# Layer 2 linear attention: the reciprocals are applied channel-major, and the logits turned instead

## The chip, the cores and the metric

The kernel runs on one core of one Trainium2 chip. The metric is the device time of one execution in microseconds. The core's engines work side by side, each through its own list of instructions in order, and wait for each other on semaphores: TensorE (PE) multiplies matrices and turns tiles, VectorE (DVE), ScalarE (ACT) and GpSimd (POOL) work element by element, SyncE (SP) issues DMAs. "Bank" means a bank of PSUM, into which TensorE writes; all other tiles lie in SBUF.

## The reference, cut to what matters

The kernel computes four layers, each an attention-like part and a feed-forward part. The change lies in the attention part of layer 2, a gated linear attention with 64 memory slots: 16 heads, 64 key channels, 128 value channels, batch 4, 512 tokens after the kernel's grouping (B, T = 4, 512).

```python
def _chunk_abc(q, k, v, s):
    scale = q.shape[-1] ** (-0.5)
    z = jax.lax.cumlogsumexp(s, axis=2)
    g = jnp.exp(jnp.concatenate([z[:, :, :1], z[:, :, :-1]], axis=2) - z)
    p = jnp.exp(s - z)
    ...
    def step_k(hk, x):
        q_t, k_t, p_t, g_t = x
        hk = hk * g_t[:, :, None, :] + k_t[..., None] * p_t[:, :, None, :]
        return (hk, jnp.einsum('bhk,bhkm->bhm', q_t, hk))
    _, okT = jax.lax.scan(step_k, hk0, (qT, kT, pT, gT))
    pvT = jax.nn.softmax(okT, axis=-1)
    def step_v(hv, x):
        pv_t, v_t, p_t, g_t = x
        hv = hv * g_t[..., None] + p_t[..., None] * v_t[:, :, None, :]
        return (hv, jnp.einsum('bhm,bhmv->bhv', pv_t, hv))
    _, ovT = jax.lax.scan(step_v, hv0, (pvT, vT, pT, gT))
```

With e = exp(s) and c its running sum over the tokens, p and the product of the g's are quotients of e and c. So the logits of a token are (the causal sum of q.k times e of the earlier token) divided by c of its own, for each slot; a softmax over the 64 slots follows; its result, divided by c once more, weighs e and v of the earlier tokens.

## The kernel before, in words

`layer2_abc` does 32 units, u = 0 to 31: eight pairs of heads times four batches. A unit has 512 tokens in four chunks of 128, and its two heads lie side by side: 2 x 64 slots or channels are 128 rows. "Channel-major" tiles have slots or channels in the partitions and tokens in the columns, "token-major" ones the reverse.

In unit u, TensorE's list (`unit` in the tensor block, L1289) mixes the attention of unit u with the projections of unit u+1, which are long and wait for little, and with the output of unit u-1:

- `scores`: q.k for each chunk and head, to `pab`, masked by VectorE to `sm`.
- `chunk_sums`: for three chunks the product of `k_tok` and `e_tok` (to `pc`, a whole 128x128 for both heads, of which only the two 64x64 blocks are used) and of `e_tok` and v (to a ring bank, by heads in 64-row halves). VectorE adds them up from chunk to chunk: `prefix_k` makes `hk` in six steps, `prefix_v` makes `hv`.
- projections s, k, q of u+1, then `ok`: the logits' sums, token-major, in `pc`: from `hk` the past chunks, from `sm` the own chunk.
- `turn_out` of u-1 (the gated output turned), projections v0 and v1, `emit` of u-1 (its product with Wo, which VectorE adds into x at L1479), projection g0.
- `turn_w`: the softmax's result `wt`, turned to channel-major in `pc`, projection g1, `weights` (L1257: `wT` times `eT` to `pab`, masked to `am`; L1264: `wT` times `hv`), then the transposes `kt`, `et`, `rt` of u+1, and `ov` (the own chunk's values).

The running sum of `eT` is taken by VectorE (`project_c`), then the reciprocal in two halves of 256 columns in place (`project_r`, L1423). TensorE turns the result (`rt`) and ScalarE copies it to `r_tok`. Reciprocals are used twice, both times token-major: VectorE multiplies the logits by them (L1499), and GpSimd multiplies the exponentials by them (L1102), beside VectorE's sum of the exponentials. ScalarE copies the turned weights from `pc` to `wT`.

VectorE's list in unit u is: masks of the scores, `prefix_v`, the clipping of s, `prefix_k`, the gating of u-1, the copy of kT, the running sum, the three steps of the logits, sum and reciprocal of the softmax, its multiply, a half of the reciprocals, the addition into x, the other half, two gate products, the masks of `am`, the sum of squares. Everything is in the order of this code; there is no scheduler. Three PSUM banks (`ring`) serve eleven fills per unit in turn, in `before` by the number of the fill modulo 3; `ring_free` waits for who took the fill three places ahead.

Of the kernel before, what the change touches and what calls it, by code (L numbers as in the profile page):

```python
# [21 lines left out]
ALU = mybir.AluOpType  # L22
# [964 lines left out]
def layer2_abc(nc, st, core, dram, a, w, aT, w2):  # L987
# [25 lines left out]
    rT = st.sb("rT", [P, T])  # L1013
    k_tok, e_tok, r_tok = (st.sb(n, [P, 2, NCH, P]) for n in ("k_tok", "e_tok", "r_tok"))
# [17 lines left out]
             "c_ready r_ready v_copied tanh_ready gate_ready k_turned e_turned r_turned k_tok_ready e_tok_ready "  # L1032
             "r_tok_ready scores_ready sm_ready hk_sums hk_step ok_ready hv_sums hv_step zeros logit_step ex_ready "
             "er_ready den_step wt_ready w_turned wT_ready am_sums am_ready ov_ready sq_ready ms_step rstd_ready "
# [9 lines left out]
    FILL = {n: k for k, n in enumerate("s q k v0 v1 g0 g1 kt et rt hv".split())}  # L1044
    taken_by = ("s_clipped", "q_copied", "k_copied", "v_copied", "v_copied", "gate_ready", "gate_ready",
                "k_tok_ready", "e_tok_ready", "r_tok_ready", "hv_step")
    per_unit = {"v_copied": 2, "gate_ready": 2, "hv_step": 3, "v_ready": 2, "g_ready": 2, "tanh_ready": 2, "r_ready": 2}

    def bank(name):
        return ring[FILL[name] % 3]  # L1050

# [21 lines left out]
    with nc.Block() as block:  # L1073
# [15 lines left out]
        def _(pool):  # L1089
# [35 lines left out]
        def _(pe):  # L1125
            pe.wait_ge(s["zeros"], 1)

            def ring_free(name, u):


                n = FILL[name]
                if n >= 3:
                    by = taken_by[n - 3]
                    per = per_unit.get(by, 1)

                    step = 1 if n - 3 in (FILL["v0"], FILL["g0"]) else per
                    pe.wait_ge(s[by], per * u + step)
                else:
                    if isinstance(u, int) and u == 0:
                        return  # L1140
                    by = {0: "r_tok_ready", 1: "hv_step", 2: "e_tok_ready"}[n]
                    per = per_unit.get(by, 1)

                    pe.wait_ge(s[by], per * u)

            def project_rows(name, u, k):
# [6 lines left out]
                for c in range(DC):  # L1153
                    ins = split_matmul(pe, bank(name)[:],
                                       w_in_parts.view(lambda t: w_qks(t, slot)[:, FILL[name], c, :]),
                                       a.view(lambda t: t[:, c, b * T:(b + 1) * T]),
                                       start=(c == 0), stop=(c == DC - 1))
# [36 lines left out]
            def chunk_sums(u, k):  # L1194
# [34 lines left out]
            def ok(u, k):  # L1229
                pe.wait_ge(s["sm_ready"], 2 * (u + 1))  # L1230
                pe.wait_ge(s["hk_step"], 6 * (u + 1))
                tok4 = chunks(pc[:])
                for c in range(NCH):
                    if c:
                        pe.matmul(tok4[:, c, :], qT[:, k % 2, c * P:(c + 1) * P], hk[:, c - 1, :], start=True,
                                  stop=False, skip_group_check=True)
                    for h in range(2):
                        m = slice(DK * h, DK * h + DK)
                        ins = pe.matmul(tok4[:, c, m], sm[:, h, c, :], e_tok[:, k % 2, c, m], start=(c == 0),
                                        stop=True, skip_group_check=True)  # L1240
                ins.then_inc(s["ok_ready"], 1)

# [33 lines left out]
            def part(steps, u, k):  # L1276
                for x in steps.split():
# [6 lines left out]
                    elif x == "et":  # L1284
                        turn("et", eT[:, k % 2], "e_ready", "e_turned", u)
                    else:
                        turn("rt", rT[:], "r_ready", "r_turned", u)

            def unit(u, k, first, last):  # L1289
# [12 lines left out]
                project("v0 v1")  # L1302
# [7 lines left out]
                project("kt et rt")  # L1310
                ov(u, k)

            part("s q k v0 v1 g0 g1 kt et rt", 0, 0)
            rounds(pe, unit)
            pe.wait_ge(s["r_tok_ready"], HP * B)
# [8 lines left out]
        def _(act):  # L1324
# [28 lines left out]
            def project_turned(u, k, names):  # L1353
                for x, dst, n in (("kt", k_tok, "k"), ("et", e_tok, "e"), ("rt", r_tok, "r")):
# [7 lines left out]
            def unit(u, k, first, last):  # L1362
# [8 lines left out]
                act.wait_ge(s["logit_step"], 3 * (u + 1))  # L1371
# [20 lines left out]
            project_turned(0, 0, ("kt", "et", "rt"))  # L1392
# [9 lines left out]
        def _(dve):  # L1402
# [12 lines left out]
            def project_c(u, k):  # L1415

                dve.wait_ge(s["e_ready"], u + 1)
                dve.tensor_tensor_scan(rT[:], ones, eT[:, k % 2], 0.0, ALU.mult, ALU.add).then_inc(s["c_ready"], 1)

            def project_r(u, half):  # L1420
                cols = slice(half * (T // 2), (half + 1) * (T // 2))
                dve.wait_ge(s["c_ready"], u + 1)
                dve.reciprocal(rT[:, cols], rT[:, cols]).then_inc(s["r_ready"], 1)  # L1423
# [57 lines left out]
            def unit(u, k, first, last):  # L1481
# [13 lines left out]

                dve.wait_ge(s["ok_ready"], u + 1)
# [12 lines left out]
                dve.wait_ge(s["er_ready"], u + 1)  # L1509
# [2088 lines left out]
```

## Time and profile before

| | us |
|---|---|
| median of 3 runs | 2202.99 (2197.28 to 2205.3) |
| span of the profiled execution | 2195.6 |
| the 32 units of the stage, first to last `weights` | 572.2 to 1351.2 |

The profile page gives the span of the profiled execution, from its first to its last instruction; a time of its own around the span is not shown for it. The median of the runs is 7.4 us above this span, their lowest 1.7.

How to read the rows: a row of the timeline has the start in us from the span's start, the duration in us, the engine, the line of the kernel, the operation, the tile written and those read, the shape, and the number of merged instructions. A full-precision (f32) matmul appears as two records, so x16 are eight matmuls. `[0.54 <-DVE ...]` is idle time of the engine just before, and who ended it. The ends of matmuls are modelled and reach beyond the start of the next; on TensorE the distance between starts is what counts.

### The profile page before, as it was taken

What the parts mean: (1) busy time and instruction counts of PE and PEld (TensorE: products, weight loads), DVE (VectorE), ACT (ScalarE), POOL (GpSimd) and SP (SyncE); (2) the same over time, 40 slices, a digit from 0 to 9 for tenths busy, and PEclk for the clock granted to TensorE, in tenths of its full rate; (3) what the DMA queues carried; (4) which work ended last, traced back from release to release, by engine and by line L of the source; (5) the groups of instructions that cost most, each with busy time, mean ns of one, the idle gap of its engine ahead of it and who ended that gap; (6) DMA issues with size and microseconds to landing.
All of it is one profiled execution on the core that took longest, in us unless ns stands there. A gap on an engine that the chain in (4) does not pass through costs nothing. (4 is left out here: it accounts for less than half of the span.)

```text
span 2195.6 us, 35301 instructions
## 1 busy us (share of the span) xinstructions
PE 1903.1 (87%) x13120; PEld 1485.3 (68%) x13120; DVE 1384.1 (63%) x3005; ACT 710.9 (32%) x1269; POOL 610.0 (28%) x584
## 2 busy tenths in 40 slices
PE   5943669962999999999999997989997987989995
PEld 2341457741899999999999996455566876756663
DVE  4476445538777777777777776476656777533334
ACT  2231424431333333333333332235534323222221
POOL 0234725540131221222121312532332103401111
PEclk9975589985999999999999998999998996999997
DMA  9329234435000000000000100000001006111114
GB/s 324 122 75 294 83 112 150 141 113 161 1 1 23 1 23 23 1 23 1 23 1 23 32 1 1 1 1 2 2 1 51 27 1 240 69 37 48 45 47 134
DMA packets 100639, 134.96 MB, mean 61 GB/s; under 512 B 11616, under 2 KB 73980, under 8 KB 99968
## 3 DMA queue, kind: packets, MB, share of 16 engines
q1 hardware_dynamic: 89344, 102.16, 14.7%
q0 software_dynamic: 11136, 30.62, 3.9%
q8 instruction: 107, 1.75, 0.3%
q14 instruction: 52, 0.43, 0.1%
HBM read 81.94 MB, written 50.81 MB: 60 GB/s over the span
## 5 line engine op out<-in xcount | busy, mean ns | idle before, releaser
L1112 POOL TENSOR_TENSOR a_rstd<-a_ms,consts 128x8 f32<-128x8 f32 x32 | 52.3, 1635 | 384.2 <-DVE a_ms L1468 384.2
L110 PE MATMUL a_ring<-a_w_hi,l_xnT_hi 128*128 128x256 f32 x512 | 155.3, 303 | 0.0
L110 PE MATMUL a_ring<-a_w_hi,l_xnT_lo 128*128 128x256 f32 x512 | 144.7, 283 | 0.0
L110 PE MATMUL a_ring<-a_w_lo,l_xnT_hi 128*128 128x256 f32 x512 | 144.5, 282 | 0.0
L2455 POOL DMA_INDIRECT l_slots_in<-xn,f_row_of x96 | 102.7, 1069 | 93.6 <-DVE f_row_of L2749 36.9
L2982 POOL DMA_INDIRECT l_pairs_out<-f_yb,f_to_row x96 | 94.6, 985 | 101.0 <-ACT f_yb L2957 63.0
L1226 PE MATMUL a_pab<-a_w_o,a_oT 128*128 128x256 f32 x512 | 119.7, 389 | 2.4 <-ACT a_oT L1360 2.4
L1423 DVE RECIPROCAL a_rT<-a_rT 128x256 f32<-128x256 f32 x64 | 111.4, 1743 | 0.0
L1226 PEld LDWEIGHTS a_pab<-a_w_o,a_oT 128*128 128x128 f32 x512 | 100.7, 202 | 13.0 <-ACT a_oT L1360 3.2
L1467 DVE TENSOR_REDUCE a_ms<-a_on 128x8 f32<-128x1024 f32 x32 | 39.0, 1220 | 109.6 <-ACT a_on L1381 109.6
L1102 POOL TENSOR_TENSOR a_wt<-a_ex,a_r_tok 128x512 f32<-128x512 f32 x32 | 40.7, 1272 | 242.4 <-ACT a_ex L1372 242.4
L1703 PE MATMUL b_ring<-b_keys,b_qm 32*128 32x128 f32 (+2 forms) x896 | 91.5, 340 | 14.8 <-DVE b_nm L1916 9.4
L1869 ACT ACTIVATE b_work<-b_ring 128x1024 f32<-128x1024 f32 (+1 forms) x96 | 81.0, 881 | 62.3 <-PE b_ring L1710 61.3
L2876 PE MATMUL f_pgu<-f_gate_up_w,f_xT 128*128 x384 | 94.6, 390 | 7.4 <-ACT f_xT L2937 6.6
L3088 POOL DMA_INDIRECT l_pairs_out<-f_yb,f_to_row x40 | 38.4, 959 | 216.0 <-ACT f_yb L3170 216.0
L110 PEld LDWEIGHTS a_ring<-a_w_lo,l_xnT_hi 128*128 128x128 f32 x512 | 97.7, 191 | 0.8
L110 PEld LDWEIGHTS a_ring<-a_w_hi,l_xnT_hi 128*128 128x128 f32 x512 | 97.6, 191 | 0.6
L110 PEld LDWEIGHTS a_ring<-a_w_hi,l_xnT_lo 128*128 128x128 f32 x512 | 97.4, 190 | 0.0
L1703 PEld LDWEIGHTS b_ring<-b_keys,b_qm 32*128 32x128 f32 x896 | 65.4, 194 | 45.0 <-issue 21.2
L319 PE MATMUL n_turned<-consts,xn 128*128 128x128 f32 x96 | 24.9, 396 | 79.6 <-DVE xn L288 79.6
L3007 DVE TENSOR_TENSOR f_gu<-f_pgu,f_bias 128x256 f32<-128x256 f32 x96 | 40.8, 425 | 78.1 <-issue 46.6
L1350 ACT ACTIVATE a_th<-a_ring 128x512 f32<-128x512 f32 x64 | 38.2, 597 | 155.1 <-PE a_ring L110 155.1
(497 smaller groups left out, 5302.8 us busy)
## 6 DMA issues: line engine op xcount, KB each, us to landing
l_slots_in<-l_zeros SPq DMA_DIRECT2D x4, 3120.0 KB, 22.8
f_xb<-l_slots_in SPq DMA_DIRECT2D x11, 1040.0 KB
f_gate_up_w<-l_pairs_out SPq DMA_DIRECT2D x16, 512.0 KB, 8.7
l_slots_in<-l_zeros SPq DMA_DIRECT2D x4, 1300.0 KB, 15.8
f_xb<-l_slots_in SPq DMA_DIRECT2D x40, 130.0 KB
f_down_w<-L_ffn_w_down_dram SPq DMA_DIRECT2D x1, 4096.0 KB
f_gate_w<-L_ffn_w_dram SPq DMA_DIRECT2D x2, 2048.0 KB
f_up_w<-L_ffn_w_dram SPq DMA_DIRECT2D x2, 2048.0 KB
```

The costliest lines, as they stand in the source:

```text
L110: ins = pe.matmul(out, a, b, start=start and k == 0, stop=stop and k == 2, **kw)
L1102: pool.tensor_tensor(wt[:], ex[:], r_tok[:, k % 2], ALU.mult).then_inc(s["er_ready"], 1)
L1112: pool.tensor_tensor(rstd[:], ms[:], core.consts[:, C_HALF:C_HALF + 8], ALU.pow).then_inc(s["rstd_ready"], 1)
L1226: ins = pe.matmul(pyy[:, t, :], cols, w_o[:, slot, h, :], start=(h == 0), stop=(h == 1))
L1423: dve.reciprocal(rT[:, cols], rT[:, cols]).then_inc(s["r_ready"], 1)
L1467: do(dve.reduce_sum(ms[:], sq[:].rearrange("t h c v -> t (h c) v"), AX.X))
L1703: return pe.matmul(ps[:, i, at:at + k1 - k0], qm[strip(j), p, c, b * T + q * P:b * T + (q + 1) * P], keys[strip(j), p, c, b * T + k0:b * T ...
L1869: act.activation(probs[:, g % 2, 2 * pair:2 * pair + 2, T_AT[k]:T_AT[k] + w], slot["t", g, pair, k][:, :, 0:w], ACT.Exp).then_inc(s["exp_r ...
L2455: pool.indirect_dma_start(self.xs[:, :], bass.IndirectOffsetOnAxis(ap=self.row_of[:, k, t:t + 1], axis=0), core.rows[:, t, :], None).then_ ...
L2876: ins = pe.matmul(pgu[:, i % 2, j * 2 * I:(j + 1) * 2 * I], xT[:, i % 2, (j * DC + c) * P:(j * DC + c + 1) * P], r.gate_up[:, bass.ds(e, 1 ...
L2982: pool.indirect_dma_start(r.ys[:, :], bass.IndirectOffsetOnAxis(ap=r.to_row[:, b:b + 1], axis=0), yb[:, i % YR, j, :], None).then_inc(stor ...
L3007: dve.tensor_tensor(gu[:, i % GR, j].rearrange("p k i -> p (k i)"), pgu[:, i % 2, j * 2 * I:(j + 1) * 2 * I], r.bias[:, bass.ds(e, 1), :, ...
```

## The change

The reciprocals stay channel-major (`rT`, now in two buffers) and are never turned: `rt`, its copy and `r_tok` go. The logits are formed channel-major, so the operands of each product in `ok` change places; three products with `hk` come first, then eight half-width ones. VectorE multiplies the result by `rT` in this form (`lgT`), TensorE turns it back into `pc` (`turn_logits`, between v0 and v1), and the maximum and the subtraction read `pc`. GpSimd's multiply goes; the softmax's result is multiplied by the reciprocals only after it has been turned, by VectorE, in the place of ScalarE's copy to `wT`. The chunk sums of k are done by heads, 64x64 each. The ring banks are assigned by name.

```diff
@@ the banks
-    FILL = {n: k for k, n in enumerate("s q k v0 v1 g0 g1 kt et rt hv".split())}
+    BANK = {"hv": 0, "s": 1, "k": 2, "q": 0, "v0": 1, "v1": 2, "g0": 0, "g1": 1, "kt": 2, "et": 0}
+    BEFORE = {"s": ("gate_ready", 2, 0, 0), "k": ("k_tok_ready", 1, 0, 0), "q": ("hv_step", 3, 0, 0),
+              "v0": ("s_clipped", 1, 1, 1), "v1": ("k_copied", 1, 1, 1), "g0": ("q_copied", 1, 1, 1),
+              "g1": ("v_copied", 2, 1, 1), "kt": ("v_copied", 2, 2, 1), "et": ("gate_ready", 2, 1, 1)}
...
@@ gpsimd
-                pool.wait_ge(s["ex_ready"], u + 1)
-                pool.wait_ge(s["r_tok_ready"], u + 1)
-                pool.tensor_tensor(wt[:], ex[:], r_tok[:, k % 2], ALU.mult).then_inc(s["er_ready"], 1)
@@ tensor, chunk_sums
                 for c in range(3):
-                    ins = pe.matmul(pc[:, c * P:(c + 1) * P], k_tok[:, k % 2, c, :], e_tok[:, k % 2, c, :],
-                                    start=True, stop=True)
+                    for h in range(2):
+                        m = slice(DK * h, DK * h + DK)
+                        ins = pe.matmul(pc[m, c * P + DK * h:c * P + DK * h + DK], k_tok[:, k % 2, c, m],
+                                        e_tok[:, k % 2, c, m], start=True, stop=True)
@@ tensor, ok
-                tok4 = chunks(pc[:])
+                for c in range(1, NCH):
+                    pe.matmul(pc[:, c * P:(c + 1) * P], hk[:, c - 1, :], qT[:, k % 2, c * P:(c + 1) * P],
+                              start=(c == 1), stop=False, skip_group_check=True)
                 for c in range(NCH):
-                    if c:
-                        pe.matmul(tok4[:, c, :], qT[:, k % 2, c * P:(c + 1) * P], hk[:, c - 1, :], start=True,
-                                  stop=False, skip_group_check=True)
                     for h in range(2):
                         m = slice(DK * h, DK * h + DK)
-                        ins = pe.matmul(tok4[:, c, m], sm[:, h, c, :], e_tok[:, k % 2, c, m], start=(c == 0),
-                                        stop=True, skip_group_check=True)
+                        ins = pe.matmul(pc[m, c * P:(c + 1) * P], e_tok[:, k % 2, c, m], sm[:, h, c, :], start=False,
+                                        stop=(c == NCH - 1), skip_group_check=True)
                 ins.then_inc(s["ok_ready"], 1)
+
+            def turn_logits(u):
+                pe.wait_ge(s["lgT_ready"], u + 1)
+                for t in range(NCH):
+                    ins = pe.transpose(pc[:, t * P:(t + 1) * P], lgT[:, t * P:(t + 1) * P], core.ident)
+                ins.then_inc(s["lg_turned"], 1)
@@ tensor, unit
-                project("v0 v1")
+                project("v0")
+                turn_logits(u)
+                project("v1")
...
-                project("kt et rt")
+                project("kt et")
@@ scalar, unit
-                copy("w_turned", u + 1, wT[:], pc[:], "wT_ready")
...
-                    project_turned(n, kn, ("kt", "et", "rt"))
+                    project_turned(n, kn, ("kt", "et"))
@@ vector, unit
-                dve.wait_ge(s["r_tok_ready"], u + 1)
-                do = Steps(dve, s["logit_step"], 3 * u, 3)
-                do(dve.tensor_tensor(lg[:], chunks(pc[:]), r_tok[:, k % 2], ALU.mult))
-                do(dve.tensor_reduce(mx[:], heads8(lg[:]), AX.X, ALU.max))
-                do(dve.tensor_tensor(heads8(lg[:]), heads8(lg[:]), mx[:].unsqueeze(2).to_broadcast([P, 8, DK]),
+                dve.tensor_tensor(lgT[:], pc[:], rT[:, k % 2], ALU.mult).then_inc(s["lgT_ready"], 1)
+                if not last:
+                    project_r(n, kn, 0)
+                dve.wait_ge(s["lg_turned"], u + 1)
+                do = Steps(dve, s["logit_step"], 2 * u, 2)
+                do(dve.tensor_reduce(mx[:], heads8(chunks(pc[:])), AX.X, ALU.max))
+                do(dve.tensor_tensor(heads8(lg[:]), heads8(chunks(pc[:])), mx[:].unsqueeze(2).to_broadcast([P, 8, DK]),
                                      ALU.subtract))
...
-                dve.wait_ge(s["er_ready"], u + 1)
-                dve.tensor_tensor(heads8(wt[:]), heads8(wt[:]), den[:].unsqueeze(2).to_broadcast([P, 8, DK]),
+                dve.tensor_tensor(heads8(wt[:]), heads8(ex[:]), den[:].unsqueeze(2).to_broadcast([P, 8, DK]),
                                   ALU.mult).then_inc(s["wt_ready"], 1)
-                if not last:
-                    project_r(n, 0)
                 if not first:
                     emit(u - 1, (k - 1) % PER)
                 if not last:
-                    project_r(n, 1)
+                    project_r(n, kn, 1)
+                dve.wait_ge(s["w_turned"], u + 1)
+                dve.tensor_tensor(wT[:], pc[:], rT[:, k % 2], ALU.mult).then_inc(s["wT_ready"], 1)
+                if not last:
                     project_g(n, kn, 0)
                     project_g(n, kn, 1)
```

Where the instructions stand. TensorE in the middle of the stage, from `turn_w` to `turn_out`, of before (the projections, all of line L110, are left out here but for their place in the words behind):

```order
L1246 MATMUL a_pc<-consts,a_wt 128x128 x4
...
L1178 MATMUL a_ring<-consts,a_kT 128x128 x4
L1178 MATMUL a_ring<-consts,a_eT 128x128 x4
L1178 MATMUL a_ring<-consts,a_rT 128x128 x4
L1272 MATMUL a_pde<-a_v,a_am 128x128 x8
L1190 MATMUL a_pab<-a_qT,a_kT 128x128 x8
L1201 MATMUL a_pc<-a_e_tok,a_k_tok 128x128 x3
L1208 MATMUL a_ring<-a_v,a_e_tok 64x128 x6
```

The same place of the changed kernel, and on through `ok`, `turn_out` and the new turn of the logits:

```order
L1169 MATMUL a_ring<-consts,a_kT 128x128 x4
L1169 MATMUL a_ring<-consts,a_eT 128x128 x4
L1270 MATMUL a_pde<-a_v,a_am 128x128 x8
L1181 MATMUL a_pab<-a_qT,a_kT 128x128 x8
L1194 MATMUL a_pc<-a_e_tok,a_k_tok 64x64 x6
L1201 MATMUL a_ring<-a_v,a_e_tok 64x128 x6
...
L1226 MATMUL a_pc<-a_qT,a_hk 128x128 x3
L1231 MATMUL a_pc<-a_sm,a_e_tok 64x128 x8
L1210 MATMUL a_pde<-consts,a_on 128x128 x8
...
L1238 MATMUL a_pc<-consts,a_lgT 128x128 x4
```

The third turn is gone from between `et` and `ov`; a turn of the same size stands after the twelve matmuls of v0. VectorE from the running sum to the gate products, of before:

```order
L1418 SCALAR_TENSOR_TENSOR a_rT<-consts,a_eT 128x512
L1499 TENSOR_TENSOR a_lg<-a_pc,a_r_tok 128x512
L1500 TENSOR_REDUCE a_mx<-a_lg 128x8
L1501 TENSOR_TENSOR a_lg<-a_lg,a_mx 128x512
L1506 TENSOR_REDUCE a_den<-a_ex 128x8
L1507 RECIPROCAL a_den<-a_den 128x8
L1510 TENSOR_TENSOR a_wt<-a_wt,a_den 128x512
L1423 RECIPROCAL a_rT<-a_rT 128x256
L1479 TENSOR_TENSOR x<-a_pab,x 128x1024
L1423 RECIPROCAL a_rT<-a_rT 128x256
L1428 SCALAR_TENSOR_TENSOR a_gate<-a_th,a_ring 128x512 x2
```

The same in the changed kernel:

```order
L1415 SCALAR_TENSOR_TENSOR a_rT<-consts,a_eT 128x512
L1496 TENSOR_TENSOR a_lgT<-a_pc,a_rT 128x512
L1421 RECIPROCAL a_rT<-a_rT 128x256
L1501 TENSOR_REDUCE a_mx<-a_pc 128x8
L1502 TENSOR_TENSOR a_lg<-a_pc,a_mx 128x512
L1507 TENSOR_REDUCE a_den<-a_ex 128x8
L1508 RECIPROCAL a_den<-a_den 128x8
L1510 TENSOR_TENSOR a_wt<-a_ex,a_den 128x512
L1477 TENSOR_TENSOR x<-a_pab,x 128x1024
L1421 RECIPROCAL a_rT<-a_rT 128x256
L1517 TENSOR_TENSOR a_wT<-a_pc,a_rT 128x512
L1426 SCALAR_TENSOR_TENSOR a_gate<-a_th,a_ring 128x512 x2
```

The first half of the reciprocals moved ahead of the maximum, and the multiply that fills `wT` stands behind the second half and ahead of the gate products.

## Rows read from the trace of the kernel before

**Rows 1.** Busy time by stretch: busy us (instructions) by engine, clock, DMA.

```profile
570.00:1350.00 780.00, 775.00 (x6336) 711.57 (x6336) 584.29 (x943) 266.89 (x406) 179.37 (x101) 0.99 0.04 12
1338.00:1347.00 9.00, 7.80 (x32) 6.95 (x32) 7.41 (x22) 1.63 (x2) 1.91 (x2) 0.50 0.00 0
1450.00:1600.00 150.00, 134.88 (x1784) 83.55 (x1788) 100.16 (x142) 79.61 (x99) 44.58 (x113) 0.99 0.01 2
```

**Rows 2.** Timeline of TensorE, first matmuls of `weights` in units 1 and 30.

```profile
597.31 1.16 PE L1257 MATMUL a_pab<-a_wT,a_eT 64*128 64x128 f32 x16
...
1325.56 1.16 PE L1257 MATMUL a_pab<-a_wT,a_eT 64*128 64x128 f32 x16
```

**Rows 3.** Timeline of TensorE, 940 to 966 us, a unit in the middle.

```profile
942.04 3.62 PE L1226 MATMUL a_pab<-a_w_o,a_oT 128*128 128x256 f32 x16
...
946.92 0.60 PE L1246 MATMUL a_pc<-consts,a_wt 128*128 128x128 f32 x4
...
948.87 1.16 PE L1257 MATMUL a_pab<-a_wT,a_eT 64*128 64x128 f32 x16
...
951.56 0.60 PE L1178 MATMUL a_ring<-consts,a_rT 128*128 128x128 f32 x4
952.00 1.95 PE L1272 MATMUL a_pde<-a_v,a_am 128*128 128x128 f32 x16
953.88 1.16 PE L1190 MATMUL a_pab<-a_qT,a_kT 64*128 64x128 f32 x16
954.97 0.94 PE L1201 MATMUL a_pc<-a_e_tok,a_k_tok 128*128 128x128 f32 x6
955.84 0.88 PE L1208 MATMUL a_ring<-a_v,a_e_tok 128*64 128x128 f32 x12
956.64 0.51 PE L110 MATMUL a_ring<-l_xnT_hi,a_w_hi 128*128 128x512 f32 x1
...
960.92 0.63 PE L1239 MATMUL a_pc<-a_e_tok,a_sm 128*128 128x64 f32 x4
961.39 0.44 PE L1235 MATMUL a_pc<-a_hk,a_qT 128*128 128x128 f32 x2
...
963.40 1.05 PE L1217 MATMUL a_pde<-consts,a_on 128*128 128x128 f32 x8
964.20 0.36 PE L110 MATMUL a_ring<-a_w_hi,l_xnT_hi 128*128 128x256 f32 x1
```

**Rows 4.** Timeline of VectorE, the same stretch.

```profile
939.99 0.69 DVE L1501 TENSOR_TENSOR a_lg<-a_lg,a_mx 128x512 f32<-128x512 f32 x1
...
943.36 0.69 DVE L1510 TENSOR_TENSOR a_wt<-a_wt,a_den 128x512 f32<-128x512 f32 x1 [0.42 <-POOL a_wt L1102]
...
945.70 1.22 DVE L1479 TENSOR_TENSOR x<-a_pab,x 128x1024 f32<-128x1024 f32 x1
946.84 1.74 DVE L1423 RECIPROCAL a_rT<-a_rT 128x256 f32<-128x256 f32 x1
948.50 0.63 DVE L1428 SCALAR_TENSOR_TENSOR a_gate<-a_th,a_ring 128x512 f32<-128x512 f32 x1
...
955.04 1.22 DVE L1467 TENSOR_REDUCE a_ms<-a_on 128x8 f32<-128x1024 f32 x1 [3.55 <-ACT a_on L1381]
...
959.78 0.99 DVE L1458 TENSOR_TENSOR a_hk<-a_pc,a_hk 64x64 f32<-64x64 f32 x4
...
963.68 0.67 DVE L1499 TENSOR_TENSOR a_lg<-a_pc,a_r_tok 128x512 f32<-128x512 f32 x1
```

**Rows 5.** Timeline of all engines: before unit 0, and in unit 31.

```profile
554.94 0.66 PE L1178 MATMUL a_ring<-consts,a_rT 128*128 128x128 f32 x4 [0.54 <-DVE a_gate L1428]
...
1335.88 0.99 DVE L1458 TENSOR_TENSOR a_hk<-a_pc,a_hk 64x64 f32<-64x64 f32 x4
...
1337.01 0.78 PE L1239 MATMUL a_pc<-a_e_tok,a_sm 128*128 128x64 f32 x4 [3.61 <-DVE a_hk L1458]
```

More of the change, by code:

```diff
@@ L1012, in layer2_abc @@
     qT, kT, eT = (st.sb(n, [P, 2, T]) for n in ("qT", "kT", "eT"))
-    rT = st.sb("rT", [P, T])
-    k_tok, e_tok, r_tok = (st.sb(n, [P, 2, NCH, P]) for n in ("k_tok", "e_tok", "r_tok"))
+    rT, lgT = st.sb("rT", [P, 2, T]), st.sb("lgT", [P, T])
+    k_tok, e_tok = (st.sb(n, [P, 2, NCH, P]) for n in ("k_tok", "e_tok"))
     v, gate = (st.sb(n, [P, 2, NCH, PV]) for n in ("v", "gate"))
@@ L1128, in ring_free @@
             def ring_free(name, u):
[L1131 to L1136, printed above, removed]
-                    pe.wait_ge(s[by], per * u + step)
[L1138 to L1144, printed above, removed]
+                by, per, step, own = BEFORE[name]
+                if own or u:
+                    pe.wait_ge(s[by], per * u + step)
             def project_rows(name, u, k):
@@ L1283, in part @@
                         turn("kt", kT[:, k % 2], "k_copied", "k_turned", u)
-                    elif x == "et":
+                    else:
                         turn("et", eT[:, k % 2], "e_ready", "e_turned", u)
-                    else:
-                        turn("rt", rT[:], "r_ready", "r_turned", u)
             def unit(u, k, first, last):
@@ L1309, in unit @@
                 weights(u, k)
-                project("kt et rt")
+                project("kt et")
                 ov(u, k)
-            part("s q k v0 v1 g0 g1 kt et rt", 0, 0)
+            part("s q k v0 v1 g0 g1 kt et", 0, 0)
             rounds(pe, unit)
-            pe.wait_ge(s["r_tok_ready"], HP * B)
+            pe.wait_ge(s["gate_ready"], 2 * HP * B)
             for t in rn.of(0):
@@ L1353, in project_turned @@
             def project_turned(u, k, names):
-                for x, dst, n in (("kt", k_tok, "k"), ("et", e_tok, "e"), ("rt", r_tok, "r")):
+                for x, dst, n in (("kt", k_tok, "k"), ("et", e_tok, "e")):
                     if x in names:
@@ L1370, in unit @@
                     project_v(n, kn, 0)
-                act.wait_ge(s["logit_step"], 3 * (u + 1))
+                act.wait_ge(s["logit_step"], 2 * (u + 1))
                 act.activation(ex[:], lg[:], ACT.Exp).then_inc(s["ex_ready"], 1)
@@ L1391, in _ @@
             project_g(0, 0, 1)
-            project_turned(0, 0, ("kt", "et", "rt"))
+            project_turned(0, 0, ("kt", "et"))
             rounds(act, unit)
@@ L1417, in project_c, with project_r @@
                 dve.wait_ge(s["e_ready"], u + 1)
-                dve.tensor_tensor_scan(rT[:], ones, eT[:, k % 2], 0.0, ALU.mult, ALU.add).then_inc(s["c_ready"], 1)
-            def project_r(u, half):
+                dve.tensor_tensor_scan(rT[:, k % 2], ones, eT[:, k % 2], 0.0, ALU.mult, ALU.add
+                                       ).then_inc(s["c_ready"], 1)
+            def project_r(u, k, half):
                 cols = slice(half * (T // 2), (half + 1) * (T // 2))
                 dve.wait_ge(s["c_ready"], u + 1)
-                dve.reciprocal(rT[:, cols], rT[:, cols]).then_inc(s["r_ready"], 1)
+                dve.reciprocal(rT[:, k % 2, cols], rT[:, k % 2, cols]).then_inc(s["r_ready"], 1)
             def project_g(u, k, half):
@@ L1527, in _ @@
             project_c(0, 0)
-            project_r(0, 0)
-            project_r(0, 1)
+            project_r(0, 0, 0)
+            project_r(0, 0, 1)
             project_g(0, 0, 0)
```

14 lines of the change are left out of this document (7 added, 7 removed).

## The prediction

> **What bounds the kernel now.** I read four views: the table of stretches for the whole layer 2 attention stage, one line's starts from unit to unit, then TensorE's rows and VectorE's rows of one unit in the middle. The stretches say what sets the pace [rows 1]: from 570 to 1350 us TensorE is busy 775.0 of 780.0 us at a granted clock of 0.99, that is the 2.4 GHz level, VectorE 584, ScalarE 267, GpSimd 179. The starts of the `weights` matmuls say how steady it is [rows 2]: 597.31 for unit 1, 1325.56 for unit 30, so 29 periods in 728.25 us, 25.11 us each. A unit's wait or saving therefore counts some 30 times (unit 0 to unit 30), and the ends by themselves.
>
> I write W for the start of `weights` in a unit (948.87) and give times as W plus something. TensorE's rows [rows 3] stand back to back: W+3.13 turn of `rT` ends (952.00), W+5.01 `ov` ends, W+12.05 `ok` starts, W+14.53 it ends, W+18.28 `emit` starts (942.04 plus a period), W+25.11 next W. VectorE [rows 4] runs without a gap from the sum of squares (955.04) to the logits, and has idle time elsewhere. Two places where it nearly holds TensorE: its last `hk` step ends at 960.77 and `ok` starts at 960.92. In the last unit, where TensorE really waits for that step, the start comes 0.14 us after it (1336.87 to 1337.01) [rows 5], so the 0.15 here is the same latency: `ok` starts when VectorE lets it, and TensorE arrives at the same moment. The other place is `emit`: its last matmul ends at 945.66, VectorE's addition into x starts at 945.70, 0.04 us later.
>
> **The change, part by part, per unit.**
>
> *Reciprocals not turned.* Four transposes go from TensorE: 951.56 to 952.00, 0.44 us, before `ov`, so all that follows moves up by 0.44, VectorE's chain too, since that starts from `ov`. The ScalarE copy of them goes too, on an engine with two thirds of its time free: nothing.
>
> *Chunk sums in 64-column tiles.* Three full matmuls took 0.87 us (954.97 to 955.84); six half ones take between half of the neighbouring `hv` sums' 0.80 us (six matmuls with 128 moving columns) and all of it, and one change of tile shape goes: 0.1 to 0.4 us less. It is worth nothing on the path: `ok` waits for the `hk` step, which is 0.14 us behind a VectorE chain that starts at ScalarE's squares and runs without a gap; TensorE only waits a little at `ok`. The bound on the other side: 0.1 us a unit if the 0.14 is not all latency.
>
> *Logits formed channel-major.* Before, 960.92 to 963.40, 2.48 us, with the weights of 64-column products loaded in full width and three switches to the `hk` products. Now three full products and eight that write half the output partitions. The full ones at the rate of `ov`, 1.88 us for eight (952.00 to 953.88), cost 0.70. The half ones have exactly the shape of the `hv` sums, 128*64 by 128x128, whose six take 0.80, change of shape behind them included; two more at the pace inside a run, 0.11 each, give 1.02, and the change ahead of them about 0.09. Sum 1.81, saving 0.67. Bounds: 1.6 if no change of shape costs, 2.6 if the halves do not overlap (8 x 0.235 + 0.70).
>
> *Logits turned back.* Four transposes, priced like those removed: 0.44, added between `v0` and `v1`. What they wait for: VectorE's multiply starts where the old one did, W+14.81, less 0.44, at W+14.37, since the scan ahead of it is the binding thing. It takes 0.67 from PSUM as the old one did, so the turn may start at W+15.1. TensorE gets there at 11.61+1.81+0.80 (`turn_out`)+1.48 (half of the 2.95 us of `v0 v1`) = W+15.70. No wait, with 0.6 us of cover.
>
> *The softmax chain.* Behind the multiply now stands half the reciprocals (1.74), then the maximum and the subtraction from PSUM, 0.69 us each as the present ones: subtraction done by 15.04+1.66+0.72+0.72, about W+18.1. The old distance from there to the weights' multiply was 2.68 us (940.68 to 943.36) and held GpSimd's product, for which VectorE waited 0.42 at the end; the product goes. Even at the old distance `wt` is done at W+21.5 (18.1+2.68+0.69), and `turn_w` stands at 23.17 (946.92 plus a period) less 0.67, W+22.5. One microsecond of cover. So the freed GpSimd work is worth nothing either.
>
> *The second multiply by the reciprocals, at `wT`.* This is where the saving is lost. The copy of the turned weights leaves ScalarE, where it ran beside VectorE's reciprocals, and becomes a VectorE multiply that stands behind the addition into x and the second half of the reciprocals. The addition can't start before `emit` is done. From the end of the last `emit` matmul: 0.04 to the addition, 1.14 to the reciprocals behind it (945.70 to 946.84), 1.66 to the next instruction (946.84 to 948.50), 0.67 for the multiply from PSUM, 0.14 to TensorE: 3.65 us. TensorE's own work from that point to `weights` is 948.87 less 945.66, 3.21 us. It waits 0.44 us in every unit. What is queued behind it on TensorE is all the next unit needs; behind the multiply on VectorE stand the two gate products and the masks of `am`. Two gates and one mask at 0.69 each, from the multiply's end at W'-0.14, give W'+1.9 for the first mask, `ov` asks for it at W'+2.69 (952.00 less 948.87 less the 0.44): covered.
>
> The Trainium skill, "VectorE: DVE Perf Modes", section on the TRN2 errata, gives VectorE 120 cycles of fixed cost from PSUM against 58 from SBUF, an argument against this move. The rows contradict it: 0.67 us from PSUM (963.68), 0.69 from SBUF alone (943.36), the same 512 elements. By the page's difference (62 cycles, an estimate of 0.06 us over the SBUF row) the wait would be about 0.53 and the time about 2198.
>
> **The sum.** TensorE's own work changes by -0.44 - 0.67 + 0.44 = -0.67 and it waits 0.44: -0.23 us a unit, over 30 periods -6.9. At the start the turn of `rT` waited for the gate, 0.54 idle and 0.66 of its own at 554.94 [rows 5], and goes: 1.2 us. Unit 0 begins those 1.2 and the 0.67 of `ok` earlier, but has no `emit` to hide VectorE's softmax chain, which has half the reciprocals more (1.66) and the wait for GpSimd less (0.42): -1.2 - 0.67 + 1.66 - 0.42 = -0.6. In the last unit VectorE sets most of the end as before; I give it -0.1. Together -7.6 us on the profiled execution's 2195.6 us span. The page shows no other time of that execution; the median of three runs is 7.4 us above its span, so I carry the difference over: 2203.0 - 7.6 = 2195.4.
>
> **Rivals.**
> *No wait at `wT`.* If the addition into x or the reciprocals start 0.44 us sooner than the rows let them, all of 0.67 stays: 30 x 0.67 + 0.7 = 21 us, 2182. For it: 0.44 us in a chain of five terms is not much, and the two latencies stand on one row each. Against: the three long terms are durations of this trace, in a row, on an in-order engine.
> *The half-width products don't overlap, slower than before.* In `ok` both halves accumulate onto a bank that the full-width `hk` products have begun. If such pairs run one behind the other, `ok` takes 2.6 to 2.7 us, 0.85 more than forecast, and the period is 25.11 - 0.23 + 0.85: 30 x 0.62 - 0.7 = +18, 2221. It becomes slower than before from an `ok` of about 2.05 us up. For it: the shape has not been seen with accumulation in this kernel. Against: the `hv` sums write one bank in halves, six in 0.80 us, while full products of the same size take 0.235 each.
> *The clock.* In the last unit the clock fell to 0.50 (the 1.2 GHz level) after 3.61 us without work [rows 1, 5]. If 0.44 us a unit did that, every unit would lose some 4 us. Against: from 1450 to 1600 us TensorE idles 15 of 150 us, at 0.99 [rows 1].
> *More waits on VectorE.* If the multiply of the logits came 0.6 us later than computed, the turn would wait too; each 0.1 beyond costs 3 us.
>
> **How the numbers follow.** Forecast 0.64, its own range 2190 to 2199. No wait 0.16. Pairs in series 0.10. Clock or a further wait 0.10, of which half stays within the next bound. Three runs of a kernel here span 8 us, so about 0.5%, 11 us, is what can be told from no change. Faster by more than that: the no-wait case and a fifth of all for a forecast whose wait is half as long, 0.36. Slower: pairs in series and most of the last case, 0.17. Within: 0.47. The range leaves out a tenth on either side: 2181 to 2208.
>
> **What would show it.** The period of the `weights` line: 24.88 us. TensorE idle before `weights`, ended by VectorE's `wT` multiply, 0.4 us in each unit; no such idle at the turn of the logits. `ok` from its first `hk` product to `turn_out` 1.8 us. A small wait at `ok` on `hk`, as long as the chunk sums got shorter. The multiply at `wT` 0.67 us, starting as the second half of the reciprocals ends. Clock 0.99 throughout. Wrong if `ok` lasts over 2 us, if `wT` does not come last before `weights`, or if the wait stands at `turn_logits`.

## The result, and the profile after

| | before | after |
|---|---|---|
| median of 4 runs, us | 2203.99 (2197.28 to 2205.3) | 2192.93 (2190.69 to 2193.66) |
| span of the profiled execution, us | 2195.6 | 2192.1 |
| period of a unit, us | 25.11 | 24.84 |

The ratio of the times is 0.9949, 95% interval 0.9936 to 0.9962: 11 us faster, about 8 to 14. Forecast was 2195.4, within 2181 to 2208.

The two spans differ by 3.5 us only, and that needs a word first. The time of an execution of either kernel lies 1.5 to 1.7 us above its own span (the profiled one of after: 2193.66 against 2192.1). So the profiled execution of the kernel before, with its span of 2195.6, fits its fastest time, 2197.28, and most of the 7.4 us between that span and the median is scatter between executions. The stage with the change (from the load of the norm's weights to the first instruction of the next stage) took 836.5 us before and 825.6 after, 10.9 less. But the stage began at 541.2 us in the trace of before and at 549.2 in that of after, behind layers that the change doesn't touch. Over all ten kernels profiled for this case the start lies between 541 and 556 us whatever the edit (table below). So a comparison of two traces goes by the stage, never by the span. The same scatter widens the intervals of the first four experiments: of 27 executions of the kernel before that ran beside them, eight took 2195.7 to 2199.9 us and nineteen 2204.5 to 2214.3.

The table of stretches of the kernel after, whole stage and last unit (columns as in rows 1):

```profile
577.00:1345.00 768.00, 744.43 (x6509) 669.33 (x6508) 595.96 (x970) 236.81 (x343) 140.22 (x70) 0.99 0.04 13
1335.00:1344.00 9.00, 8.54 (x40) 7.08 (x41) 6.93 (x19) 1.67 (x2) 1.64 (x1) 0.50 0.00 0
```

TensorE is no longer busy all the time: 23.6 us of 768 are idle, where it was 5.0 of 780 [rows 1]. The clock is the same, 0.99, the 2.4 GHz level. The first `weights` matmuls of units 1 and 30:

```profile
603.59 1.16 PE L1255 MATMUL a_pab<-a_wT,a_eT 64*128 64x128 f32 x16 [0.24 <-DVE a_wT L1517]
...
1323.94 1.16 PE L1255 MATMUL a_pab<-a_wT,a_eT 64*128 64x128 f32 x16 [0.23 <-DVE a_wT L1517]
```

29 periods in 720.35 us, 24.84 each, against 25.11 [rows 2], and each of the two rows has the idle time that the prediction asked for, ended by VectorE's `wT` multiply, though it is 0.24 us and not 0.4. TensorE in a unit in the middle:

```profile
951.35 1.16 PE L1255 MATMUL a_pab<-a_wT,a_eT 64*128 64x128 f32 x16 [0.24 <-DVE a_wT L1517]
...
954.04 1.95 PE L1270 MATMUL a_pde<-a_v,a_am 128*128 128x128 f32 x16
955.92 1.16 PE L1181 MATMUL a_pab<-a_qT,a_kT 64*128 64x128 f32 x16
957.01 0.57 PE L1194 MATMUL a_pc<-a_e_tok,a_k_tok 128*64 128x64 f32 x12
957.41 0.83 PE L1201 MATMUL a_ring<-a_v,a_e_tok 128*64 128x128 f32 x12
958.17 0.50 PE L110 MATMUL a_ring<-l_xnT_hi,a_w_hi 128*128 128x512 f32 x1
...
962.96 0.91 PE L1226 MATMUL a_pc<-a_qT,a_hk 128*128 128x128 f32 x6 [0.38 <-DVE a_hk L1456]
963.79 1.09 PE L1231 MATMUL a_pc<-a_sm,a_e_tok 128*64 128x128 f32 x16
964.82 1.09 PE L1210 MATMUL a_pde<-consts,a_on 128*128 128x128 f32 x8
965.67 0.36 PE L110 MATMUL a_ring<-a_w_hi,l_xnT_hi 128*128 128x256 f32 x1
...
967.18 0.60 PE L1238 MATMUL a_pc<-consts,a_lgT 128*128 128x128 f32 x4
...
969.04 3.62 PE L1219 MATMUL a_pab<-a_w_o,a_oT 128*128 128x256 f32 x16
...
973.92 0.60 PE L1244 MATMUL a_pc<-consts,a_wt 128*128 128x128 f32 x4
...
976.18 1.05 PE L1255 MATMUL a_pab<-a_wT,a_eT 64*128 64x128 f32 x14 [0.24 <-DVE a_wT L1517]
```

Times from W = 951.35, beside those of [rows 3]: `ov` ends at 4.57 (5.01), `ok` starts at 11.61 (12.05), ends at 13.47 (14.53), `emit` starts at 17.69 (18.28), next W at 24.83 (25.11). The chunk sums take 0.40 us (957.01 to 957.41) where they took 0.87, and `ok` starts exactly as far from `ov` as it did, 7.04 us: the time saved there has become a wait of about half a microsecond, of which the row shows 0.38 as idle. There is none at the turn of the logits (967.18). VectorE in the same unit:

```profile
961.82 0.99 DVE L1456 TENSOR_TENSOR a_hk<-a_pc,a_hk 64x64 f32<-64x64 f32 x4
...
965.72 0.66 DVE L1496 TENSOR_TENSOR a_lgT<-a_pc,a_rT 128x512 f32<-128x512 f32 x1
966.30 1.74 DVE L1421 RECIPROCAL a_rT<-a_rT 128x256 f32<-128x256 f32 x1
967.96 0.63 DVE L1501 TENSOR_REDUCE a_mx<-a_pc 128x8 f32<-128x512 f32 x1
968.62 0.69 DVE L1502 TENSOR_TENSOR a_lg<-a_pc,a_mx 128x512 f32<-128x512 f32 x1
...
971.03 0.69 DVE L1510 TENSOR_TENSOR a_wt<-a_ex,a_den 128x512 f32<-128x512 f32 x1
972.70 1.23 DVE L1477 TENSOR_TENSOR x<-a_pab,x 128x1024 f32<-128x1024 f32 x1 [0.97 <-PE a_pab L1219]
973.84 1.74 DVE L1421 RECIPROCAL a_rT<-a_rT 128x256 f32<-128x256 f32 x1
975.50 0.63 DVE L1517 TENSOR_TENSOR a_wT<-a_pc,a_rT 128x512 f32<-128x512 f32 x1
```

The three VectorE instructions behind `emit` read as the prediction wrote them [rows 4 for before]: the addition at 972.70 after 0.97 idle, reciprocals at 973.84 (1.14 later), the multiply at 975.50 (1.66 later), 0.63 long, and TensorE starts at 976.18. The multiply of the logits starts at W+14.37, as forecast.

### The profile page after: what moved, and what is told of

Same layout as the page of the kernel before. It is cut to its first block and busy times, and to the rows that moved or that the text cites. A ratio compares the mean times of both kernels' runs of the same rounds, so it can differ in the third digit from the quotient of the medians.

```text
span 2192.1 us, 35525 instructions
## 1 busy us (share of the span) xinstructions
PE 1875.1 (86%) x13312; PEld 1444.0 (66%) x13312; DVE 1399.3 (64%) x3037; ACT 680.2 (31%) x1205; POOL 565.3 (26%) x552
## 5 line engine op out<-in xcount | busy, mean ns | idle before, releaser
L110 PE MATMUL a_ring<-a_w_hi,l_xnT_hi 128*128 128x256 f32 x512 | 157.3, 307 | 0.0
L110 PE MATMUL a_ring<-a_w_hi,l_xnT_lo 128*128 128x256 f32 x512 | 144.2, 282 | 0.0
L110 PE MATMUL a_ring<-a_w_lo,l_xnT_hi 128*128 128x256 f32 x512 | 144.0, 281 | 0.0
L110 PEld LDWEIGHTS a_ring<-a_w_lo,l_xnT_hi 128*128 128x128 f32 x512 | 97.2, 190 | 0.8
L110 PEld LDWEIGHTS a_ring<-a_w_hi,l_xnT_hi 128*128 128x128 f32 x512 | 97.0, 189 | 0.8 <-issue 0.2
L110 PEld LDWEIGHTS a_ring<-a_w_hi,l_xnT_lo 128*128 128x128 f32 x512 | 96.8, 189 | 0.0
L1711 PE MATMUL b_ring<-b_qm,b_keys 32*128 32x384 f32 (+3 forms) x512 | 86.9, 461 | 0.0
## 6 DMA issues: line engine op xcount, KB each, us to landing
f_gate_w<-L_ffn_w_dram SPq DMA_DIRECT2D x2, 2048.0 KB, 11.1
```

Of the source, the lines that this page charges most:

```text
L110: ins = pe.matmul(out, a, b, start=start and k == 0, stop=stop and k == 2, **kw)
L1711: return pe.matmul(ps[:, i, at:at + T - kb * P], keys[strip(j), p, c, b * T + kb * P:b * T + (kb + 1) * P], qm[strip(j), p, c, b * T + kb ...
```

## The experiments

All kernels are compared with the kernel before. after_again, e1, e4 and e2 ran together on one chip, e5, e3, e6 and e7 together on another. The start and length of the stage and the period (the distance between two `weights`, mean of 29) are read from each kernel's trace, in us. But for e5's, the intervals of the ratios overlap, so the conclusions rest on period and stage.

| kernel | stage starts | period | stage | time, us | ratio to before |
|---|---|---|---|---|---|
| before | 541.2 | 25.11 | 836.5 | | |
| after | 549.2 | 24.84 | 825.6 | 2192.9 | 0.9949 (0.9936 to 0.9962) |
| after_again | 555.2 | 24.84 | 825.3 | 2196.9 | 0.9954 (0.9924 to 0.9984) |
| e1_r_ahead | 541.9 | 24.53 | 815.9 | 2188.9 | 0.9925 (0.9896 to 0.9954) |
| e4_clip_behind | 555.5 | 24.29 | 808.4 | 2182.8 | 0.9901 (0.9865 to 0.9938) |
| e2_full_sums | 549.3 | 24.84 | 826.6 | 2198.4 | 0.9962 (0.9933 to 0.9991) |
| e5_both | 548.6 | 23.99 | 799.1 | 2167.9 | 0.9835 (0.9822 to 0.9849) |
| e3_before_half_sums | 548.5 | 25.13 | 837.4 | 2205.3, one run | |
| e6_wT_first | 549.3 | 24.77 | 823.4 | 2192.6, one run | |
| e7_pool | 549.3 | 24.85 | 825.7 | 2193.9, one run | |

**The changed kernel again** (after_again), no edit.

> The changed kernel once more, as the measure for the others of this chip. Period of the weights line 24.84 us as before in its trace, the stage from its first DMA to the next stage's first instruction 825.7 us. Open: its total against the kernel before. The stage alone is 10.9 us shorter in the two traces, while the spans differ by 3.5 us only, because the changed kernel's stage began 8.1 us later. If the late start was chance, the ratio comes out near 0.995 again; if the change causes it (another place of code or tiles), the stage starts late again, near 549 us, in this trace and the ratio stays near 0.998 to 0.995.

Period 24.84, stage 825.3, ratio 0.9954. The late start doesn't come from the change: e3, the kernel before with one edit, starts at 548.5, and e1, with the change, at 541.9. What lies behind the stage is 817 to 818 us in nine of the ten traces (815 in e2), so in the traces it is the part ahead of the stage that varies. TensorE spent 207 us of that part at the lower level of its clock (0.50) in the two traces that start the stage earliest, 214 to 227 in the six that start it near 549, and 225 and 240 in the two near 555. The two go together, though not in strict order; which is the cause isn't shown. The waits of TensorE in this kernel, over 22 units (who waited, for whom, us in total, times, longest):

```profile
PEld a_pab L1255 <- DVE a_wT L1517: 9.6, 22, 0.4
PE a_pc L1226 <- DVE a_hk L1456: 8.4, 22, 0.4
...
PE a_pab L1255 <- DVE a_wT L1517: 5.2, 22, 0.2
```

**The second half of the reciprocals ahead of the addition** (e1_r_ahead).

```diff
-                if not first:
-                    emit(u - 1, (k - 1) % PER)
                 if not last:
                     project_r(n, kn, 1)
+                if not first:
+                    emit(u - 1, (k - 1) % PER)
                 dve.wait_ge(s["w_turned"], u + 1)
```

> The changed kernel with the second half of the reciprocals ahead of the addition into x on VectorE, nothing else. Theory (TensorE waits 0.30 us a unit at weights because addition, reciprocals and the multiply stand in a row on VectorE behind emit): the reciprocals fill the 0.97 us in which VectorE idles before the addition, the multiply ends about 0.9 us earlier, the wait at weights goes, period 24.53 to 24.56, about 9 us less than the changed kernel. Rival (the gap at weights is a fixed cost, a change of tile shape or semaphore latency behind g1): period stays 24.84, time the same. Second rival (the addition, 0.7 us later, now holds weights, which waits for it too): period 24.9 or more.

Period 24.53, the theory's number; the stage 9.3 to 9.7 us shorter than in the two traces of the changed kernel, the median 8 us lower. Two successive `weights` rows, no idle time ahead of either:

```profile
939.84 1.16 PE L1255 MATMUL a_pab<-a_wT,a_eT 64*128 64x128 f32 x16
...
964.37 1.16 PE L1255 MATMUL a_pab<-a_wT,a_eT 64*128 64x128 f32 x16
```

And of the two waits only the one for `hk` is left in the list of waits:

```profile
PE a_pc L1226 <- DVE a_hk L1456: 9.5, 23, 0.4
```

So the gap at `weights` was the row of work on VectorE, 0.31 us of it in each unit, neither a fixed cost of TensorE nor the addition alone. The multiply itself got no faster; it stands behind the addition now and takes 0.69 us where it took 0.63:

```profile
963.06 0.69 DVE L1517 TENSOR_TENSOR a_wT<-a_pc,a_rT 128x512 f32<-128x512 f32 x1
```

**Clipping behind the hk steps** (e4_clip_behind).

```diff
+                prefix_k(u)
                 if not last:
                     project_s(n, kn)
-                prefix_k(u)
```

> The changed kernel with the clipping of s behind the six hk steps on VectorE instead of ahead of them. Theory (the shorter chunk sums are lost at ok, where TensorE waits 0.5 us for hk): the hk steps end 0.61 us earlier, ok starts 0.45 to 0.5 us earlier, period 24.34 to 24.40, about 14 us less than the changed kernel. The wait at weights stays at 0.30, since emit moves with it. Rival (ok waits for something else, the masks or the projections): period 24.84. Rival that gives a part back: the exponential and the running sum come later, the multiply of the logits too, and TensorE waits at the turn of the logits: period 24.5 to 24.8.

Period 24.29, 0.55 less, a little more than expected; stage 17 us shorter, the median 14. The start of `ok` moves from W+11.61 to W+11.08. The wait at `ok` is gone from the list, the one at `weights` stays:

```profile
PE a_pab L1255 <- DVE a_wT L1517: 5.4, 23, 0.2
```

The queue ahead of `hk` on VectorE was what `ok` waited for. The same queue stood there in the kernel before; it cost nothing visible, because TensorE arrived at the same moment.

**Full chunk sums** (e2_full_sums), the change without one of its parts.

```diff
                 for c in range(3):
-                    for h in range(2):
-                        m = slice(DK * h, DK * h + DK)
-                        ins = pe.matmul(pc[m, c * P + DK * h:c * P + DK * h + DK], k_tok[:, k % 2, c, m],
-                                        e_tok[:, k % 2, c, m], start=True, stop=True)
+                    ins = pe.matmul(pc[:, c * P:(c + 1) * P], k_tok[:, k % 2, c, :], e_tok[:, k % 2, c, :],
+                                    start=True, stop=True)
```

> The changed kernel with the chunk sums of k as before, three full 128x128 products. Theory (halving them is hidden by the hk steps): TensorE's chunk sums take 0.87 us instead of 0.40, the start of ok moves by 0.05 at most, period 24.84 to 24.90, time the same within 2 us. Rival (the halved sums made the gain): period 25.3, 14 us slower than the changed kernel and about the time of the kernel before.

Period 24.84, unchanged, and the median within the 2 us (2198.4 against 2196.9). The rows of one unit (start at W = 952.86): the sums take 0.87 again, and `ok` starts at W+11.61 as with the halved ones, without idle time ahead of it.

```profile
952.86 1.16 PE L1253 MATMUL a_pab<-a_wT,a_eT 64*128 64x128 f32 x16 [0.23 <-DVE a_wT L1515]
...
958.52 0.94 PE L1192 MATMUL a_pc<-a_e_tok,a_k_tok 128*128 128x128 f32 x6
959.39 0.88 PE L1199 MATMUL a_ring<-a_v,a_e_tok 128*64 128x128 f32 x12
...
964.47 0.91 PE L1224 MATMUL a_pc<-a_qT,a_hk 128*128 128x128 f32 x6
```

**Halved chunk sums alone in the kernel before** (e3_before_half_sums), the same edit the other way round, by itself.

> The kernel before with one part of the change alone, the chunk sums of k by heads as 64x64 products. Theory (ok of the kernel before starts 0.14 us after the last hk step, which is this wait's latency, so it is VectorE that sets it): TensorE's chunk sums take 0.40 us instead of 0.87, it waits the difference at ok, period 25.05 to 25.12. Rival (TensorE was the bound there, the two coincided by chance and the latency is shorter, 0.05 us): up to 0.1 us less, 25.01. Rival (halving is a gain by itself): 24.65.

Period 25.13, 0.02 more than before and 0.01 above the theory's range. The sums are 0.5 us shorter and `ok` waits for VectorE, W+12.06 (W+12.05 before):

```profile
956.51 1.16 PE L1259 MATMUL a_pab<-a_wT,a_eT 64*128 64x128 f32 x16
...
962.61 0.57 PE L1203 MATMUL a_pc<-a_e_tok,a_k_tok 128*64 128x64 f32 x12
...
968.57 0.63 PE L1241 MATMUL a_pc<-a_e_tok,a_sm 128*128 128x64 f32 x4 [0.41 <-DVE a_hk L1460]
```

Together with e2 this settles that part of the change: it is worth nothing in either kernel. The kernel before was held by VectorE at this point, by a hair.

**Both moves** (e5_both): the edits of e1 and e4 together in the changed kernel.

> The changed kernel with both moves: the clipping of s behind the hk steps, and the second half of the reciprocals ahead of the addition into x. Theory (two separate waits, 0.3 us at weights and 0.5 us at ok, one VectorE queue behind each): the gains add, period 24.84 - 0.31 - 0.55 = 23.98, up to 24.1, stage 25 us shorter than the changed kernel's 825.5, some 800, and about 37 us less than the kernel before. Rival (the waits are one, moved about: TensorE then waits for VectorE at a third place, the turn of the logits or the turn of the softmax's weights): period 24.2 to 24.3, no better than the better one of the two alone.

Period 23.99, stage 799.1; ratio 0.9835 to the kernel before, 37 us faster. The savings add up (24.84 - 0.31 - 0.55 = 23.98), so the two waits were separate. TensorE's rows of one unit, two `weights` and what is between them at the places of the former waits, without idle time:

```profile
938.45 1.16 PE L1255 MATMUL a_pab<-a_wT,a_eT 64*128 64x128 f32 x16
...
944.51 0.83 PE L1201 MATMUL a_ring<-a_v,a_e_tok 128*64 128x128 f32 x12
...
949.49 0.89 PE L1226 MATMUL a_pc<-a_qT,a_hk 128*128 128x128 f32 x6
...
962.44 0.83 PE L1255 MATMUL a_pab<-a_wT,a_eT 64*128 64x128 f32 x10
```

Here the halved chunk sums should count, though no run has them full in this kernel: the 4.98 us from the `hv` sums to `ok` (944.51 to 949.49) are their own 0.76 and the 4.22 of the projections. TensorE sets the pace again, but barely: `ok` starts 0.17 us after the last `hk` step ends (948.33 + 0.99 = 949.32), where 0.15 was the distance when it had to wait.

**The multiply at wT ahead of the second half** (e6_wT_first).

```diff
-                if not last:
-                    project_r(n, kn, 1)
                 dve.wait_ge(s["w_turned"], u + 1)
                 dve.tensor_tensor(wT[:], pc[:], rT[:, k % 2], ALU.mult).then_inc(s["wT_ready"], 1)
                 if not last:
+                    project_r(n, kn, 1)
                     project_g(n, kn, 0)
```

> The changed kernel with the second half of the reciprocals behind the multiply that fills wT, instead of ahead of it. Theory (the wait at weights is the row addition, half reciprocals, multiply): the multiply is done before TensorE asks, the wait at weights goes, but the 1.66 us stand ahead of the gate products and the masks now, the first mask ends 2.9 us after weights begins or later, and ov, which asks for it at 2.69, waits 0.2 to 0.5 us. Period 24.7 to 25.0: the wait has moved. Rival (masks have cover enough): period 24.53, as with the reciprocals ahead of the addition.

Period 24.77, within the theory's range: `ov` starts at W+2.83 instead of 2.69, and lasts 0.10 longer for its second mask, 0.24 in all (24.53 + 0.24 = 24.77). The wait has moved, as the list shows; VectorE waits for the turned weights, and TensorE's weight loads for the mask:

```profile
DVE a_wT L1515 <- PE a_pc L1244: 14.7, 23, 0.6
...
PEld a_pde L1270 <- DVE a_am L1433: 4.6, 22, 0.2
```

**GpSimd's multiply back, without use** (e7_pool).

```diff
+                pool.wait_ge(s["ex_ready"], u + 1)
+                pool.wait_ge(s["e_tok_ready"], u + 1)
+                pool.tensor_tensor(lg[:], ex[:], e_tok[:, k % 2], ALU.mult).then_inc(s["idle_done"], 1)
...
                 dve.wait_ge(s["lg_turned"], u + 1)
+                if not first:
+                    dve.wait_ge(s["idle_done"], u)
```

> The changed kernel with GpSimd's multiply of 512 columns put back without use: it multiplies ex by e_tok and writes the result over lg, which nobody reads again. Theory (GpSimd's work was off the path and doesn't slow VectorE beside it): period 24.83 to 24.85, VectorE's sum of the exponentials beside it 0.69 us as now. Rival (part of the gain comes from a quieter GpSimd, through the memory they share): VectorE's instructions beside it longer by some per cent, and the period 24.9 or more.

Period 24.85, 0.01 more, as the theory said. But the other half of the theory, that GpSimd doesn't slow VectorE beside it, holds for one instruction and fails for the next:

```profile
971.82 1.27 POOL L1107 TENSOR_TENSOR a_lg<-a_ex,a_e_tok 128x512 f32<-128x512 f32 x1 [7.83 <-ACT a_ex L1373]
...
971.84 0.69 DVE L1512 TENSOR_REDUCE a_den<-a_ex 128x8 f32<-128x512 f32 x1 [0.76 <-ACT a_ex L1373]
...
972.80 0.84 DVE L1515 TENSOR_TENSOR a_wt<-a_ex,a_den 128x512 f32<-128x512 f32 x1
974.47 1.22 DVE L1480 TENSOR_TENSOR x<-a_pab,x 128x1024 f32<-128x1024 f32 x1 [0.83 <-PE a_pab L1222]
```

The sum, which lies wholly beside GpSimd's multiply, takes its usual 0.69 us. The multiply behind it, which overlaps GpSimd's by 0.3 us, takes 0.84 instead of 0.69 (0.836 to 0.847 in all 32 units). That costs no time here, because VectorE idles ahead of the addition: 0.83 us where it was 0.97. In the kernel before, this multiply waited for GpSimd's and could not overlap with it. So GpSimd's work was off the path in this change, but not without an effect on VectorE; in the order of e5, where VectorE doesn't idle there, it might count. That wasn't run.

## Why the prediction was right, point by point

*Who sets the pace.* Right. TensorE was the bound, and the two places named as near to VectorE (the last `hk` step, and the addition behind `emit`) head the two waits that TensorE has afterwards, at `ok` and at `weights`. e1 and e4 each remove one and leave the other.

*Reciprocals not turned: 0.44.* Measured 0.44 (`ov` ends 4.57 after W instead of 5.01). This part and the next ones are sized from the rows; no run takes them one by one.

*Chunk sums: nothing on the path, 0.1 to 0.4 shorter.* Right in effect (e2, e3). The saving of the instructions themselves was under-sized: it is 0.47, with 0.40 for the three pairs of 64x64 products where three full ones took 0.87. None of the 0.1 us that might have come through at `ok` did.

*ok: 1.81 instead of 2.48.* Measured 1.86 (962.96 to 964.82). The pairs overlap with accumulation as they do without: eight half-width products take 1.03 us. The three full ones take 0.83 rather than 0.70; in e4, where TensorE doesn't wait ahead of them, 0.77. The rival of pairs in series is out.

*Turn of the logits: 0.44, no wait.* From `turn_out`'s end to `emit` there are 3.37 us (965.67 to 969.04), 2.95 before: 0.42. No wait.

*The wait at weights: 0.44.* The mechanism is shown by e1, the size was off: 0.31. The term that was mis-sized is the last of the chain, 0.14 from VectorE's end to TensorE's start. Measured: 975.50 + 0.63 = 976.13 to 976.18, 0.05. The 0.14 came from the row at `ok`, and it is still 0.15 there (961.82 + 0.99 = 962.81 to 962.96). The trace of after offers a reason. Each of the two places waits for two semaphores, the second of them in an instruction of its own ahead of the first weight load (32 and 31 times, 51 ns each):

```profile
L1224 PEldq EVENT_SEMAPHORE  x32: 51/51/51, 568.2 to 1334.9; - x32
...
L1251 PEldq EVENT_SEMAPHORE  x31: 51/51/51, 601.4 to 1348.0; - x31
```

At `ok` that instruction (L1224, 0.05 us) waits for `hk`, the one that comes last, and the weight load follows behind it. At `weights` it (L1251) waits for the addition into x, which is long done, and the weight load itself waits for `wT`. The distances are 0.15 and 0.05 us in every unit that waits; no run changed the order of the two semaphores, so this cause is argued and not shown. The multiply was also 0.04 shorter than its term. Against this stand 0.05 each at `ok` and at `turn_out`.

*The sum.* -0.27 us a unit instead of -0.23: 30 periods make -8.2 (572.2 to 1325.56 is 753.4; in the trace of after 745.2), forecast -6.9.

*The ends.* Forecast -0.6 and -0.1; the stage's remaining difference is -2.7 in the trace of after and -3.0 in after_again, so this is where most of the gap between 7.6 and 11 lies. From the stage's start to W of unit 0 there are 31.0 us before, 29.5 and 30.8 after; from unit 30 to 31 25.6 before, 24.7 and 23.2 after; behind that 26.5, and 26.3 and 26.1. Both pieces lie where the granted clock changes between its two levels. At the start the term holds within the scatter: all eight traces with the change have 29.5 to 31.0 us there. In the last unit the term of -0.1 failed. 25.6 us are the same in both kernels without the change (before, e3), and seven of the eight traces with it have 23.2 to 23.5: 2.1 to 2.4 us less, and only the trace of after has 24.7. Part of this was in the rows: the last unit also starts from an `ov` that ends 0.44 us sooner, and its `ok` starts 11.02 us after W of unit 30 (1323.94 to 1334.96), where it was 11.45 [rows 2, 5]. The rest goes with the clock: between these two `weights` it was at its lower level for 10.2 us in the three traces with 24.7 or more and for 3.4 or 6.8 in the seven others. What made the lower stretch shorter was not looked into. TensorE's first row of `ok` in unit 31, behind the last long wait of the stage, in after:

```profile
1334.96 1.62 PE L1226 MATMUL a_pc<-a_qT,a_hk 128*128 128x128 f32 x6 [4.13 <-DVE a_hk L1456]
```

and in after_again:

```profile
1342.17 0.91 PE L1226 MATMUL a_pc<-a_qT,a_hk 128*128 128x128 f32 x6 [4.13 <-DVE a_hk L1456]
```

In the trace of after the clock was 0.50 from 1335 to 1344 us, the 1.2 GHz level, as it was before [rows 1, 5]; in after_again these three products still ran at the upper level, after the same 4.13 us without work. "VectorE sets most of the end as before" left out both the earlier start and how long TensorE works at 1.2 GHz.

*How much of the agreement is luck.* The medians differ by 11.1 us and the stages by 10.9, but the part ahead of the stage moves by up to 14 us between executions, so that the medians of four agree so well with the stage is partly luck. What is right by its mechanism is the period: 8.2 us of the difference, forecast 6.9.

*The rule on PSUM.* The Trainium skill, "VectorE: DVE Perf Modes", section on the TRN2 errata, gives VectorE 120 cycles of fixed cost from PSUM against 58 from SBUF. No such difference shows in these rows. The cleanest pair is the subtraction, in the same place behind the maximum: 0.69 us from SBUF before (939.99, [rows 4]) and 0.69 with one operand in PSUM after (968.62). Nor is PSUM faster, as the prediction's 0.67 against 0.69 and the 0.63 of `wT` and of the maximum seem to say. These shorter ones start before the instruction ahead of them has ended. The `wT` multiply takes 0.63 behind a reciprocal and 0.69 behind the addition (e1), both from PSUM, and in the kernel before the first gate product takes 0.63 behind a reciprocal (948.50, [rows 4]). So the duration went with the neighbour and not with the memory.

*The other rivals.* No wait at `wT` (0.16) did not come true, but was one edit away: e1. The clock stayed at 0.99 in the stage, with 0.3 and 0.5 us of waiting in each unit, so that rival is out. There is no further wait at the turn of the logits.

## What to carry to other kernels

When the bound engine's work gets shorter, list for each of its waits when the other side will be ready, in times from a fixed point of the loop; a semaphore that cost nothing because both sides came together takes the next saving whole (0.47 us of chunk sums bought nothing, and two orders of VectorE's list changed afterwards bought 0.85 us a unit, three times what the change itself did). What a multiply costs that takes the place of a copy is set less by its own duration (0.63 us here) than by what stands ahead of it on its new engine. And of a steady loop compare the period, not the span: here the part ahead of it moves by up to 14 us from run to run.

## What the runs showed of the hardware

- Pairs of half-width products (64 stationary columns each) accumulate side by side onto one bank that full-width products have begun: eight, four pairs, in 1.03 us, against 0.235 us for each full one.
- Pairs with 64 moving columns are faster again: six in 0.40 us; the same sums as three full products take 0.87.
- The same kind of wait, VectorE to TensorE, costs 0.05 us at `weights` and 0.15 at `ok`, where the semaphore that comes last is awaited by an instruction of its own (0.05 us).
- VectorE's instructions of 512 columns take 0.69 us from SBUF and with an operand in PSUM alike; directly behind a reciprocal both the multiply and the maximum take 0.63.
- A VectorE multiply that overlaps a GpSimd multiply takes 0.84 us instead of 0.69; a VectorE sum beside the same GpSimd instruction keeps its 0.69 (e7).
- The layers ahead of the stage, whose code no edit touches, ended up to 14 us apart: the stage began between 541.2 and 555.5 us.
- The clock was at 0.99 in the stage with up to 0.5 us of waiting twice a unit; in the last unit, behind 4.13 us without work, it fell to 0.50, for 10.2 us in the trace of after and for 3.4 in that of after_again.
